# Inputs of units and batches turned by transfers and VectorE instead of TensorE; rotated keys, norm epsilon and mean sign placed on other engines

## What is computed

```python
x = x + _layernorm(attn(_layernorm(x)))
x = x + _layernorm(ffn(_layernorm(x)))
# _layernorm: (x - mean) / sqrt(var + 1e-5)
# attn: 16 heads of 128; q = x @ Wq.T; one shared key and one shared value per token (x @ Wkv.T),
#   scaled per head by a running sum of x @ Wkvh.T times exp(cumsum(log_sigmoid(x @ Wg.T)))
#   q and k rotated: [t1*cos - t2*sin, t2*cos + t1*sin]; causal softmax; o @ Wout.T
# ffn: gate, up = split(x @ ternary(w_gate_up).T); h = silu(gate) * up
#   rms_norm(h) @ ternary(w_proj).T
```

## Time and profile before

| what | us |
|---|---|
| median of 3 runs | 1040.49 |
| lowest and highest of them | 1040.42, 1040.52 |
| the profiled execution's own time | 1039.91 |
| its span in the profile | 1038.1 |
| busy in the span: PE | 1021.4 |
| POOL | 931.4 |
| ACT | 868.2 |
| DVE | 827.1 |

### The profile page before, as it was taken

The page is one execution under the profiler, slowest core; times in us unless marked ns, Lnnn a source line. Parts: engine busy times, 40 slices in busy tenths (PEclk is TensorE's granted clock), DMA queues, the critical chain, the costliest instruction groups (busy, mean ns, idle before and its releaser), DMA issues.

```text
span 1038.1 us, 25078 instructions
## 1 busy us (share of the span) xinstructions
PE 1021.4 (98%) x7827; PEld 981.6 (95%) x7827; DVE 827.1 (80%) x2841; ACT 868.2 (84%) x2399; POOL 931.4 (90%) x926
## 2 busy tenths in 40 slices
PE   7999999999999999999999999999999999999996
PEld 6899999999999999999999999999999999999996
DVE  6868888878887888788888888887777767677776
ACT  5988898989898989898989898889898867877774
POOL 4899999999999999999999999999999847877775
PEclk9999999999999999999999999999999999999998
DMA  7561121112112110121122112111131000000001
GB/s 262 187 184 43 42 63 41 43 52 68 44 36 61 63 42 33 62 63 42 33 68 67 42 39 75 43 42 53 42 113 31 2 1 11 22 24 29 22 22 41
DMA packets 35124, 58.56 MB, mean 56 GB/s; under 512 B 3136, under 2 KB 16000, under 8 KB 34688
## 3 DMA queue, kind: packets, MB, share of 16 engines
q1 hardware_dynamic: 34992, 56.96, 17.2%
HBM read 50.92 MB, written 9.18 MB: 58 GB/s over the span
## 4 chain that ended last, share of the span: by engine, by line
POOL 60%; PE 19%; issue 14%; DVE 1%; POOLq 0%; ACT 0%; ACTq 0%; DVEq 0%
POOL arena L599 15%; POOL arena L622 14%; POOL arena L633 13%; POOL arena L609 13%; PE psum L1017 12%; PE psum L1057 6%; POOL arena L581 1%; POOL arena L557 1%; POOL X L590 1%; PE psum L775 1%; PE psum L1030 1%; POOL arena L565 0%; PE psum L1039 0%; POOLq L303 0%; POOL arena L572 0%
## 5 line engine op out<-in xcount | busy, mean ns | idle before, releaser
L633 POOL TENSOR_TENSOR arena<-arena 128x768 f32<-128x768 f32 x128 | 196.2, 1533 | 8.9 <-DVE arena L1580 8.3
L609 POOL TENSOR_TENSOR arena<-arena 128x512 f32<-128x512 f32 x128 | 174.0, 1359 | 10.0
L1593 DVE SCALAR_TENSOR_TENSOR pt_split<-psum,vh_col,pt_split 128x256 fp32r<-128x256 f32 (+1 forms) x512 | 177.0, 407 | 3.5 <-ACT pt_split L1252 3.0
L599 POOL TENSOR_TENSOR arena<-arena,tables 128x512 f32<-128x512 f32 x128 | 166.9, 1304 | 13.7 <-ACT arena L1222 13.0
L622 POOL TENSOR_TENSOR arena<-arena 128x512 f32<-128x512 f32 x127 | 162.9, 1283 | 0.0
L929 PE MATMUL psum<-arena 128*128 128x256 f32 x512 | 153.9, 382 | 3.1 <-POOL arena L609 1.8
L775 PE MATMUL psum<-wo_hi,o_hi 128*128 128x256 f32 x512 | 152.1, 297 | 0.0
L1233 ACT ACTIVATE arena<-arena 128x256 f32<-128x256 f32 x256 | 128.6, 502 | 26.7 <-DVE arena L1570 20.1
L775 PE MATMUL psum<-xt_lo,wq_hi 128*128 128x256 f32 x512 | 144.7, 283 | 0.0
L775 PE MATMUL psum<-xt_hi,wq_lo 128*128 128x256 f32 x512 | 144.5, 282 | 0.0
L775 PE MATMUL psum<-wo_hi,o_lo 128*128 128x256 f32 x512 | 144.3, 282 | 0.0
(11 more groups left out here) (195 smaller groups left out, 3405.7 us busy)
## 6 DMA issues: line engine op xcount, KB each, us to landing
arena<-kh_rows SPq DMA_DIRECT2D x127, 256.0 KB, 3.3
out<-spare SPq DMA_DIRECT2D x15, 256.0 KB, 2.1
arena<-w_rows SPq DMA_DIRECT2D x6, 512.0 KB, 4.8
X<-L_attn_Wout SPq DMA_DIRECT2D x1, 2048.0 KB, 14.5
X<-L_attn_x SPq DMA_DIRECT2D x1, 2048.0 KB, 12.5
arena<-L_attn_Wq SPq DMA_DIRECT2D x1, 1536.0 KB, 10.0
X<-L_attn_x SPq DMA_DIRECT2D x1, 1536.0 KB, 9.7
w_rows<-L_ffn_w_gate_up SPq DMA_DIRECT2D x3, 512.0 KB, 8.2
```

The source lines that it names most:

```text
L599: nc.gpsimd.tensor_tensor(swap, swap, spread, ALU.mult).then_inc(q_sined, 1)
L609: nc.gpsimd.tensor_tensor(q_rot[p % 2], q_cos[p % 2], q_swap[p % 2], ALU.add).then_inc(q_roped, 1)
L633: nc.gpsimd.tensor_tensor(tb, tb, r.unsqueeze(3).to_broadcast([P, HP, 3, P]), ALU.mult).then_inc(p_ready, 1)
L1593: last = nc.vector.scalar_tensor_tensor(pt_lo[p % 2][:, o], b[:, i], vh[:, t, h:h + 1], pt_hi[p % 2][:, o].bitcast(F32), ALU.mult, ALU.sub ...
```

## The change

Four parts:

1. The input of batches 2 to 15 and of units 1 to 15 is no longer transposed by PE. ACT writes the normalised rows block by block, SP moves them with four transfers into a new tile `moved`, and DVE transposes blocks of 32x32 into `F_BANK` (`turn_x`, `turn_x2`). Batches 0 and 1 and unit 0 stay on PE.
2. The keys' sine product goes from POOL to DVE (`keys_sin`), ahead of the swap, and the halves are swapped by two transfers on SP (`k_turned` to `k_swap`) in place of two copies on ACT. The first batch's swap stays on ACT.
3. Adding epsilon and the mean's sign change for both attention norms go from POOL to ACT (`prepare_x`, `prepare_y`), two small operations each, from batch 2 on for x and for all batches for y.
4. Orders: the second half of `norm_x` comes a step earlier; in the feed-forward step ACT normalises a unit in the step of its statistics, late in the step; DVE's and ACT's `split_x2` come earlier.

The core of the diff (unchanged context and declarations are cut):

```diff
-FRONT = dict(turn=0, split=0, ..., gates_one=2, key_swap=2, key_cos=3, key_sin=3, key_rope=4,
+FRONT = dict(move=-1, turn=0, split=0, ..., gates_one=2, key_cos=3, key_swap=3, key_rope=4,
-AHEAD = dict(stats_a=3, stats_b=4, invert=5, norm_a=6, norm_b=7)
+AHEAD = dict(stats_a=3, stats_b=4, invert=5, norm_a=6, norm_b=6, move=7)
-FLAG = dict(stats=0, norm=1, turn=1, up=2, sum=3, down=3, z=3, out=4)
+FLAG = dict(stats=0, norm=0, turn=1, up=2, sum=3, down=3, z=3, out=4)
...
+        moved_in = moved[:, :].rearrange("p (a g c) -> p g a c", a=4, c=P // 4)
+        turned_out = F_BANK.rearrange("p (g q a) -> p g a q", a=4, q=P // 4)
...
 SP
+            def spread_blocks(rows, landed):
+                flat = rows.rearrange("p t e -> p (t e)")
+                for b in range(4):
+                    sp.dma_start(moved[b * 32:(b + 1) * 32, :].rearrange("q (a g) -> q a g", a=4),
+                                 flat[:, b * P:(b + 1) * P]).then_inc(landed, 16)
...
+                    c0 = front_at(g0, s, "move")
+                    if c0 is not None:
+                        sp.wait_ge(ln1_done, c0 + PAIRS)
+                        at_least(sp, xt_turned, c0)
+                        spread_blocks(xn, x_moved)
+                    c0 = front_at(g0, s, "key_swap")
+                    if c0 is not None:
+                        sp.wait_ge(k_sin_done, c0 + PAIRS)
+                        at_least(sp, k_ready, c0)
+                        sp.dma_start(k_swap[0:D // 2, :], k_turned[D // 2:D, :]).then_inc(k_swapped, 16)
+                        sp.dma_start(k_swap[D // 2:D, :], k_turned[0:D // 2, :]).then_inc(k_swapped, 16)
...
-            with sp.Fori(0, BATCH - 3, 2) as u:
-                for i in range(2):
-                    rows = out_rows[:, bass.ds(address((u + i) * NT), NT), :]
-                    sp.wait_ge(res_done, u + i + 1)
-                    sp.dma_start(rows, res[i]).then_inc(stored[i], 16)
+            def move_x2(u):
+                sp.wait_ge(x2_norm, u * NT + NT)
+                sp.wait_ge(x2_turned, u)
+                spread_blocks(x2_rows(u, u % 2), x2_moved)
+            for u in range(1, 4):
+                move_x2(u)
+            for u in range(BATCH - 2):
+                sp.wait_ge(res_done, u + 1)
+                sp.dma_start(out_rows[:, u * NT:(u + 1) * NT, :], res[u % 2]).then_inc(stored[u % 2], 16)
+                if u + 4 < BATCH:
+                    move_x2(u + 4)
 POOL
...
-                nc.gpsimd.tensor_tensor(k_swap, k_swap, sink, ALU.mult).then_inc(k_sin_done, PAIRS)
...
-                pool.wait_ge(k_sin_done, c0 + PAIRS)
+                pool.wait_ge(k_swapped, (c0 + PAIRS) * 32 // PAIRS)
...
-                nc.gpsimd.tensor_tensor(ln2_rstd, ln2_agg[:, :, 1], eps[:, 0:1].to_broadcast([P, NT]), ALU.add)\
-                    .then_inc(ln2_eps, PAIRS)
-                nc.gpsimd.tensor_tensor(ln2_minus, ln2_agg[:, :, 0], minus_one, ALU.mult).then_inc(ln2_neg, PAIRS)
 PE
...
-                if at and at[0] > 0:
-                    turn_x2(*at)
...
-                    if c0 is not None:
+                    if c0 == PAIRS:
                         turn_x(c0, 1 - par)
 ACT
+            def prepare_x(c0):
+                act.wait_ge(ln1_aggr, c0 + PAIRS)
+                at_least(act, ln1_done, c0)
+                nc.scalar.activation(ln1_rstd, ln1_agg[:, :, 1], ACT.Identity, bias=eps[:, 0:1]).then_inc(ln1_eps, PAIRS)
+                nc.scalar.activation(ln1_minus, ln1_agg[:, :, 0], ACT.Copy, scale=-1.0).then_inc(ln1_neg, PAIRS)
...
-                nc.scalar.activation(k_swap[0:D // 2, :], F_BANK[D // 2:D, 0:N], ACT.Copy).then_inc(k_swapped, PAIRS // 2)
-                nc.scalar.activation(k_swap[D // 2:D, :], F_BANK[0:D // 2, 0:N], ACT.Copy).then_inc(k_swapped, PAIRS // 2)
...
+                    if u > 0:
+                        o, i_ = by_rows(x2_rows(u, i), t), by_blocks(i_)
 DVE
+            def turn_x(c0):
+                dve.wait_ge(x_moved, (c0 // PAIRS - 1) * 64)
+                dve.wait_ge(vh_copied, c0)
+                dve.wait_ge(v_lo_done, c0)
+                if chunks_turned(c0):
+                    dve.wait_ge(wt_copied, ROUND + ROUND * chunks_turned(c0))
+                nc.vector.transpose(turned_out, moved_in).then_inc(xt_turned, PAIRS)
...
+            def keys_sin(c0):
+                dve.wait_ge(gate_exp, c0 + PAIRS)
+                at_least(dve, k_swapped, c0 * 32 // PAIRS)
+                nc.vector.tensor_tensor(k_turned, F_BANK[:, 0:N], sink, ALU.mult).then_inc(k_sin_done, PAIRS)
...
+            def turn_x2(u):
+                dve.wait_ge(x2_moved, u * 64)
+                dve.wait_ge(x2_lo_done, u)
+                nc.vector.transpose(turned_out, moved_in).then_inc(x2_turned, 1)
```

More of the change, by code:

```diff
@@ L109, in sandwich_kernel @@
         eps = sb("eps", [P, 1])
+        moved = sb("moved", [P, NT * E])
         cosq, sinq, cosk, sink = (tables[:, i, :] for i in range(4))
@@ L549, in invert_x @@
             def invert_x(c0):
[L551 to L554, removed]
-                nc.gpsimd.tensor_tensor(ln1_minus, ln1_agg[:, :, 0], minus_one, ALU.mult).then_inc(ln1_neg, PAIRS)
+                if c0 <= PAIRS:
+                    pool.wait_ge(ln1_aggr, c0 + PAIRS)
+                    at_least(pool, ln1_done, c0)
+                    nc.gpsimd.tensor_tensor(ln1_rstd, ln1_agg[:, :, 1], eps[:, 0:1].to_broadcast([P, NT]), ALU.add)\
+                        .then_inc(ln1_eps, PAIRS)
+                    nc.gpsimd.tensor_tensor(ln1_minus, ln1_agg[:, :, 0], minus_one, ALU.mult).then_inc(ln1_neg, PAIRS)
                 pool.wait_ge(ln1_eps, c0 + PAIRS)
@@ L1338, in step @@
                     activate(*at, 1)
+                at = unit_at(u0, s, FLAG["up"])
+                if at:
+                    high_hidden(*at, 1)
+                    square_hidden(*at, 0)
+                    square_hidden(*at, 1)
+                at = unit_at(u0, s, FLAG["turn"])
+                if at and at[0] > 0:
+                    split_x2(*at)
+                at = unit_at(u0, s, FLAG["up"])
+                if at:
+                    activate(*at, 2)
+                    high_hidden(*at, 2)
+                    activate(*at, 3)
+                    square_hidden(*at, 2)
                 at = unit_at(u0, s, FLAG["norm"])
@@ L1343, in step @@
                 if at:
-                    high_hidden(*at, 1)
-                    square_hidden(*at, 0)
-                    square_hidden(*at, 1)
-                    activate(*at, 2)
-                at = unit_at(u0, s, FLAG["turn"])
-                if at and at[0] > 0:
-                    split_x2(*at)
-                at = unit_at(u0, s, FLAG["up"])
-                if at:
-                    high_hidden(*at, 2)
-                    activate(*at, 3)
-                    square_hidden(*at, 2)
                     high_hidden(*at, 3)
@@ L1362, in batch @@
                     exponent(g0, s)
+                    c0 = front_at(g0, s, "invert")
+                    if c0 is not None and c0 > PAIRS:
+                        prepare_x(c0)
+                    c0 = tail_at(g0, s, "invert")
+                    if c0 is not None:
+                        prepare_y(c0)
                     first_silu(g0, s)
@@ L1767, in step @@
                     multiply(*at, 1)
+                at = unit_at(u0, s, FLAG["turn"])
+                if at and at[0] > 0:
+                    turn_x2(at[0])
                 at = unit_at(u0, s, FLAG["z"])
@@ L1802, in batch @@
                     weights_finish(g0, s)
+                    c0 = front_at(g0, s, "turn")
+                    if c0 is not None and c0 > PAIRS:
+                        turn_x(c0)
                     c0 = front_at(g0, s, "split_lo")
```

50 lines of the change are left out of this document (24 added, 26 removed).

## The result

The changed kernel takes 1059.79 us (median of 5 runs, 1059.10 to 1060.98), against 1040.49 for the kernel before beside it. The ratio is 1.0188 [1.0176, 1.0200]: slower by 1.9%. The forecast was 1041.6 us with a range of 1035 to 1050, so the direction was among its cases, and the time lies 9.8 us above the upper end of the range.

The account below looks back on a forecast made before the run. PE was taken to set the pace before; after the change a circuit over SP's store and moves would bound most feed-forward units. Attention -6.6 and feed-forward +7.7 gave +1.1 on 1040.49: 1041.6 us, range 1035 to 1050.

Parts of the forecast that it names:

- attention, to the last score: Attention part: 6.0 us less from PE's transposes and 0.6 from fewer waits for POOL, -6.6 us in all.
- hand-over to the first M: Between attention's last score and the feed-forward part's first third multiply; the forecast had no term for it.
- M: Feed-forward part: the start of the third `multiply` of a step, from which the forecast counts a unit's times.
- first two periods (forecast: units 1 to 3): Feed-forward units whose moves wait for no store: bounded by ACT and DVE at 12.3 us, +0.13 x 3 = +0.4 us.
- twelve units behind a store: Feed-forward units 4 to 15: 12.73 us each instead of 12.17, +6.7 us, plus 0.6 for late landings.
- the circuit over SyncE: Feed-forward: add_x, store, four moves, landing, DVE's transpose and statistics in a row, 12.73 us from M to M.
- the forecast's other circuit: Feed-forward: the circuit of ACT and DVE, 12.3 us a unit; as sole bound, a rival of 1035.9 us, chance 0.18.
- the dear wait: Rival, feed-forward at `turn_x2`: landing 2.1, transpose 1.0, 13.7 us a unit, 1053 us; case put at 1048, chance 0.26.
- GpSimd's relief: Attention: POOL loses the sine product and four small operations per batch, so PE's waits shrink by 0.6 us (0 to 1.8).
- POOL is not the pace: Attention: POOL does not set the pace, PE's waits for it being 1.8 us; its relief counts only 0.6 us.
- The reading that PE sets it: Kernel before, both stages: PE is always busy and sets the pace, a feed-forward unit taking 12.17 us.
- The forecast's 1047 by that rule: Feed-forward moves: with the page's fixed 2.0 us per transfer, twelve steps are 0.5 us longer, time about 1047.

Follow-up runs that it names:

- E1: The changed kernel with SyncE issuing the four moves of unit u+4 ahead of the store of unit u; 1037.91 us.
- E4: The changed kernel with each unit move carrying the same 64 KB as 32 rows of 2 KB, not 128 pieces of 512 bytes; 1055.88 us.
- E11: The changed kernel with only the first two of a unit's four moves, half of the rows not moved; 1043.60 us.
- E5: E1 with the statistics and inversion of unit 1 taken one step earlier, ahead of the hand-over; 1035.76 us.
- E6: E1 with every unit's statistics taken one unit earlier, in VectorE's gap behind add_squares; 1028.44 us.
- E7: The kernel before with only the batches' inputs turned by four moves and VectorE's transpose; 1037.55 us.
- E10: E7 plus the norm's preparation moved to ScalarE, keys' rotation as before the change; 1033.43 us.
- E12: The changed kernel with units turned by TensorE as before, and every unit's statistics taken one unit earlier; 1033.11 us.
- E8: The kernel before with only the keys' rotation changed: sine product on VectorE, halves swapped by two transfers; 1039.57 us.

## Why the prediction was wrong

| step | predicted | measured |
|---|---|---|
| attention, to the last score | -6.6 | -7.2 |
| hand-over to the first M | 0 | +3.6 |
| first two periods (forecast: units 1 to 3) | +0.4 | -0.4 |
| twelve units behind a store | +7.3 | +23.7 |
| the last period | 0 | -0.6 |

*The mechanism was right.* The forecast named the circuit over SyncE. In it `add_x` ends at M+5.70 (predicted 5.70), and the transpose to the next M takes 3.61 (0.61 + 3.02 predicted). E1 shows the mechanism by removing it, and what is left, 12.27, is the forecast's other circuit (12.3).

*Two terms of the circuit over SP were mis-sized, both down: the issue of the four moves and their landing.* The last move is issued at M+8.11, not 7.57: I took 0.43 for an issue from two key spreads, and a move takes 0.60 and starts 0.64 behind its neighbour. The landing is 2.2, not 1.5: I chose the value between a 16 KB row of 1.4 and a 256 KB row of 2.1 near the small end, as if bytes set it. E4 shows that the size and shape of the pieces hardly matter, and E11 goes with a price per transfer. Together 0.54 + 0.67 = 1.2 us a unit, over 14 in twelve. The regular unit takes 13.93, not 12.73. The forecast's own rival, the dear wait, said 13.7 and 1053 us and had 0.26; I then put the case at 1048, between its ends, and the range stopped at 1050, though the upper bound of the sum itself was 13.92 a unit, +21 us. Its 13.7 is near the measured 13.93 partly by luck: it had the landing right (2.1) and added 0.4 for a dear transpose. The transpose took the 0.61 of my sum, and the slower issue, which the rival did not have, took its place in the sum.

*Irregular units.* Five of the twelve take 14.36 to 15.22. In two of them one issue takes 0.98 or 1.32 us, in two the first move starts 0.5 to 0.6 late, and in one (M = 904.73) the last move is issued on time and lands after 3.5 us instead of 2.2. Together they are 3.5 us over the regular 13.93; I had allowed 0.6. The last of the twelve is 1.1 shorter. The granted clock does not explain them: the unit from 904.73, the longest, had 1.00, and the one from 947.82 took a regular 13.92 at 0.88. What lengthens the five was not tried.

*A step was missing.* I counted unit 1 as unhindered, since no store stands ahead of its moves. But it is the first, and its chain from statistics to transpose starts only near the hand-over; with transposes on TensorE it was shorter by the four moves and the landing. Begun earlier, it gave back 1.8 us (E5) and, with every unit's statistics moved, 2.9 (E6).

*Attention: right sum, wrong account.* I gave 6.0 to TensorE's transposes and 0.6 to GpSimd's relief. E7 gives 2.4 for the turn alone, and the preparation brings 4.1 more (E10). The sum came out because part 3 of the change relieved GpSimd in the step where it delivers; the forecast had not made its 6.0 depend on that, so this much is luck. "POOL is not the pace" was true only while TensorE had its transposes; 1.8 us of waits said little, since they measured the state before. GpSimd was idle for 27 of 715 us, 1.9 in a batch and more than the 0.43 that TensorE lost, but such a share does not say in which step the room is.

*The pace before.* The reading that PE sets it held: the period stays 12.17 with the circuit of ACT and DVE shortened (E12), and in attention relieving GpSimd of the keys' product alone gave no difference that can be told (E8).

The Trainium skill (DMA: Bandwidth & Descriptors, section Anatomy of one DMA — SWDGE (gpsimd) path) has a fixed cost of about 2.0 us for a transfer issued by GpSimd. The 64 KB moves' 2.2 and 2.0 agree with it, though they are issued by SyncE; the 16 KB transfer's 1.4 does not. The forecast's 1047 by that rule was nearer than its sum. The forecast's estimate of 1.2 us for the transpose, worked out from a figure of the Trainium skill (VectorE: DVE Perf Modes, section The three transpose paths), does not agree: the transpose took 0.73, with the next operation 0.64 behind.

## What to carry to other kernels

Before putting a transfer between two engines' steps, write down what stands ahead of it on its queue and when that is released: here the order of two statements is worth 21.8 us, and the moves could have started 2.8 us earlier in a unit. Give a small transfer a price of its own whatever it carries, take the largest of the neighbouring landings, and multiply the issue by the count. Work taken off the engine that sets the pace shows only as far as the next one is behind; look which of its short operations stand in the step where it delivers, for here they counted more than a long one elsewhere.

## What was not expected of the hardware

- Moving 64 KB within the chip's memory as 128 pieces of 512 bytes or as 32 rows of 2 KB costs nearly the same: issue 0.60 against 0.59 us, landing 2.2 against 2.0 (E4).
- VectorE's transpose of 128x512 fp32 from SBUF to PSUM takes 0.73 us, hardly more than a plain operation of that shape (0.69).
- The granted clock was 0.97 in the feed-forward stretch after, where TensorE idled 12% of the time, and 1.00 in the same stretch of E1, E6 and E12. Where it fell, it cost nothing that shows: in the unit from 947.82 (0.88) TensorE was busy for 13.44 us and in the unit ahead of it (0.99) for 11.94, and the periods were 13.92 and 13.93.
- A GpSimd operation on 128x2 (L602 in E7, attention) took 0.58 to 1.10 us where it started during a VectorE operation on 128x1024 bf16, always ending just behind it, and 0.19 to 0.20 where it met none.
